# Next queries and negated maxima turned inside the running head; last gathers with fewer blankings

## What is computed

```
x = _layernorm(x + _L0_attn_ref(x, Wq, Wk, Wv, Wo))            # causal, 16 query heads on 4 key heads of 16, rope
x = _layernorm(x + _L0_xattn_ref(x, ctx, ctx, mask, ...))      # 16 heads over 64 context rows, causal
x = _layernorm(x + _L0_ffn_ref(x, ...))                        # 8 experts of 256-1024-256, top 2, and a shared one
x = _layernorm(x + _L1_attn_ref(x, time_mix_k, ...))           # K, V, R; S = scan(state * decay + K); (R * (S * first + K) * V) @ Wo
x = _layernorm(x + _L1_xattn_ref(x, ctx, ctx, mask, ...))      # one head of 256 over 64 context rows
x = _layernorm(x + _L1_ffn_ref(x, ...))                        # 16 experts of 256-128-256, top 4, and two shared ones
```

## Time and profile before

| | us |
|---|---|
| median of 3 runs | 1320.81 |
| lowest and highest | 1320.22, 1320.89 |
| the profiled execution | 1321.61 |
| its span, first to last instruction | 1319.4 |

### The profile page before, as it was taken

How to read it: one execution, slowest core, us unless ns; L and a number is a source line. 1 busy time by engine, 2 the same in 40 slices (tenths; PEclk the granted TensorE clock), 3 DMA queues, 4 the chain that set the end, 5 groups by cost and what they waited for, 6 DMA issues and landing times. The chain is left out here.

```text
span 1319.4 us, 23829 instructions
## 1 busy us (share of the span) xinstructions
PE 1157.6 (88%) x7558; PEld 836.2 (63%) x7558; DVE 697.9 (53%) x1882; ACT 586.9 (44%) x1071; POOL 474.6 (36%) x948
## 2 busy tenths in 40 slices
PE   7799898999978868999999999998789769999970
PEld 4344444444344435889999999987455556999940
DVE  4766666766255643422222323267677637554664
ACT  3277677777755634222333333231443122557710
POOL 7355332231432331013332323211342265716456
PEclk9599999999988988999999999999798759999995
DMA  9900200000000007301111111040800014867633
GB/s 347 351 1 13 86 0 1 0 0 1 1 0 1 1 1 303 150 25 34 40 37 37 37 37 39 27 136 1 274 1 1 12 69 131 259 194 240 205 118 102
DMA packets 68128, 109.32 MB, mean 83 GB/s; under 512 B 7345, under 2 KB 54962, under 8 KB 65202
## 3 DMA queue, kind: packets, MB, share of 16 engines
q1 hardware_dynamic: 58130, 80.96, 18.0%
q0 software_dynamic: 9888, 27.01, 6.4%
HBM read 65.61 MB, written 42.34 MB: 82 GB/s over the span
## 5 line engine op out<-in xcount | busy, mean ns | idle before, releaser
L1421 ACT ACTIVATE f_work<-f_bank,f_ub 128x128 f32<-128x128 f32 x312 | 89.0, 368 | 204.3 <-PE f_bank L1743 204.3
L496 ACT ACTIVATE att_PT<-att_ST 128x1024 f32<-128x1024 f32 (+1 forms) x192 | 148.1, 809 | 64.2 <-PE att_ST L634 32.7
L541 DVE CUSTOM_DVE_ANT_0 att_junk<-att_RB,att_causal_q 128x128 f32<-128x128 f32 (+3 forms) x256 | 120.7, 488 | 58.0 <-PE att_RB L616 49.0
L1743 PEld LDWEIGHTS f_bank<-f_work,f_xTf 128*128 128x128 f32 x1248 | 145.3, 192 | 3.9 <-DVE f_work L1543 2.0
L1743 PE MATMUL f_bank<-f_work,f_xTf 128*128 128x128 f32 x1248 | 145.8, 275 | 1.5 <-DVE f_work L1543 1.5
L1752 PE MATMUL f_bank<-wd_down,f_work 128*128 x624 | 141.1, 379 | 0.0
L616 PE MATMUL att_RB<-att_kT,att_qT 96*128 96x512 bf16 (+3 forms) x384 | 120.4, 351 | 22.0 <-DVE att_mx L541 6.6
L1752 PEld LDWEIGHTS f_bank<-wd_down,f_work 128*128 128x128 f32 x624 | 115.5, 190 | 14.1
L1372 POOL DMA_INDIRECT Yd<-f_work,f_inv x39 | 38.5, 987 | 196.3 <-DVE f_work L1562 196.3
L1552 DVE COPY f_xTf<-wu_up 128x1024 f32 x78 | 54.1, 695 | 102.6 <-PE f_bank L1743 94.9
L616 PEld LDWEIGHTS att_RB<-att_kT,att_qT 96*128 96x128 bf16 x384 | 34.0, 98 | 112.9 <-issue 41.2
(11 more groups left out here) (460 smaller groups left out, 2188.1 us busy)
## 6 DMA issues: line engine op xcount, KB each, us to landing
Xd<-g_zero SPq DMA_DIRECT2D x1, 12032.0 KB, 41.2
f_xin<-Xd SPq DMA_DIRECT2D x47, 256.0 KB
Yd<-f_yo SPq DMA_DIRECT2D x47, 256.0 KB, 2.6
wu_up<-up_w SPq DMA_DIRECT2D x9, 1024.0 KB, 9.3
wd_down<-down_w SPq DMA_DIRECT2D x9, 1024.0 KB, 18.4
w_all<-w SPq DMA_DIRECT2D x6, 768.0 KB, 10.6
wu_up<-Yd SPq DMA_DIRECT2D x16, 256.0 KB, 6.0
w_all<-w SPq DMA_DIRECT2D x1, 2304.0 KB, 17.2
```

What stands on the lines that cost most here:

```text
L496: act.activation(buf[:, :, 0:w], ST[:, 2 * (k % 2):2 * (k % 2) + 2, 0:w], ACT.Exp, scale=float(HD) ** -0.5).then_inc(exp_done, 1)
L541: dve.tensor_tensor_reduce(junk[:, k % RING, 0:w], RB[:, bank, 0:w], G.causal_q[:, 512 - w:512], 1.0, LOWEST, ALU.add, ALU.max, to).then_i ...
L1421: last = act.activation(hT[:, u % 2, m, :], bank[:, UB + m // 4, (m % 4) * P:(m % 4 + 1) * P], ACT.Gelu, bias=ub[:, ds(e, 1), m])
L1743: mm = pe.matmul(bank[:, UB + n, P * m:P * (m + 1)], staged_up[:, kk, at:at + P], xT[:, u % 2, kk, :], start=(kk == 0), stop=(kk == KD - 1))
```

## The change

In the prologue of the self-attention, `trQ` of the next head now stands behind the fourth `mx` of the running head, and `trm` of the head before behind its eighth. In the last head `trK` takes the place of `trQ`. At the end only `trQ` 0 and `trm` 3 are left. All `tr` steps but the first two go to two banks of their own, which are the first two of `ST`; the maxima keep the ring of three. PE waits for the two banks to be read before the iterations start, and once for the input tiles that ACT reads from there.

In the recurrent stage `ct` moves between the two halves of `r` of the last quarter, `lc` and `sx` 0 to 3 directly behind `r`. `spread_of` loses two of four operations where only `rstd` is used. In the other cases the negation comes first and is not waited for.

In the second half of the last gathers a blanking stays only behind every second gather of tiles 0 to 2, so 26 of 32 go. `spread(1)` moves from behind tile 0 to behind tile 2, and `norm(1)` on DVE from ahead of tile 1 to ahead of tile 3.

```
-    PROLOGUE += [("trQ", _r or -REP)] + [("mx", 12 * _r + k) for k in range(12)]
+    _head = [("mx", 12 * _r + k) for k in range(12)]
     if _r:
-        PROLOGUE.append(("trm", _r - 1))
-PROLOGUE += [("trK", 0), ("trm", REP - 1), ("trQ", 0)]
+        _head.insert(8, ("trm", _r - 1))
+    _head.insert(4, ("trQ", _r + 1) if _r + 1 < REP else ("trK", 0))
+    PROLOGUE += _head
+PROLOGUE += [("trQ", 0), ("trm", REP - 1)]
...
+class Prologue(Placed):
...
+            kind = "mx" if what == "mx" or n < 2 else "tr"
+            bank = turns[kind] % RING if kind == "mx" else RING + turns[kind] % SPARE
...
+                            pe.wait_ge(v_read, RINGP + NT - 2)
...
+            for n in range(RING, RING + SPARE):
+                pe.wait_ge(bank_free[n], PRO.count[n])
...
-    put(("r", 3, 1), ("ct", 0, 0))
-    put(("rs", 3, 1), ("lc", 0, 0), ("sx", 0, 3))
+    put(("r", 3, 0), ("ct", 0, 0))
+    put(("r", 3, 1), ("lc", 0, 0), ("sx", 0, 3))
...
-                ch.link(pool.tensor_tensor(rstd[n][p][:, j], rstd[n][p][:, j], half[:, j], ALU.pow))
-                ch.link(pool.tensor_tensor(shift[n][p][:, j], mv[n][p][:, j, 0], rstd[n][p][:, j], ALU.mult))
-                pool.tensor_scalar(shift[n][p][:, j], shift[n][p][:, j], -1.0, None, ALU.mult).then_inc(rstd_ready[n], 1)
+                if n == 1:
+                    pool.tensor_tensor(rstd[n][p][:, j], rstd[n][p][:, j], half[:, j], ALU.pow).then_inc(rstd_ready[n], 1)
+                else:
+                    ch.done(pool.tensor_scalar(shift[n][p][:, j], mv[n][p][:, j, 0], -1.0, None, ALU.mult))
+                    ch.link(pool.tensor_tensor(rstd[n][p][:, j], rstd[n][p][:, j], half[:, j], ALU.pow))
+                    pool.tensor_tensor(shift[n][p][:, j], shift[n][p][:, j], rstd[n][p][:, j], ALU.mult).then_inc(rstd_ready[n], 1)
...
-                        ch.pause(route.rest[:, 0:16])
-                    if n and s == 0:
+                        if n == 0 or (s < 3 and r % 2):
+                            ch.pause(route.rest[:, 0:16])
+                    if n and s == 2:
                         spread(1)
...
-                if s == 1:
+                if s == 3:
                     norm(1)
```

More of the change, by code:

```diff
@@ L172 @@
 PLAN = iteration_plan()
-PROLOGUE = [("trK", -1)]
+PROLOGUE = [("trK", -1), ("trQ", -REP)]
 for _r in range(REP):
-    PROLOGUE += [("trQ", _r or -REP)] + [("mx", 12 * _r + k) for k in range(12)]
+    _head = [("mx", 12 * _r + k) for k in range(12)]
     if _r:
-        PROLOGUE.append(("trm", _r - 1))
-PROLOGUE += [("trK", 0), ("trm", REP - 1), ("trQ", 0)]
+        _head.insert(8, ("trm", _r - 1))
+    _head.insert(4, ("trQ", _r + 1) if _r + 1 < REP else ("trK", 0))
+    PROLOGUE += _head
+PROLOGUE += [("trQ", 0), ("trm", REP - 1)]
 PLAN_6 = [x for x in PLAN if x not in (("trK", 0), ("trQ", 0))]
@@ L181 @@
 TRANSPOSES = ("trm", "trK", "trQ", "otr")
-RING = 3
+RING, SPARE = 3, 2
 class Placed:
@@ L219, in looped, with __init__ @@
     return placed
-PRO = Placed(PROLOGUE, [0] * RING)
-MID = Placed(PLAN, PRO.after())
+class Prologue(Placed):
+    def __init__(self, plan):
+        self.plan, self.base, self.at, self.count = plan, [0] * (RING + SPARE), [], [0] * (RING + SPARE)
+        turns = {"mx": 0, "tr": 0}
+        for n, (what, k) in enumerate(plan):
+            kind = "mx" if what == "mx" or n < 2 else "tr"
+            bank = turns[kind] % RING if kind == "mx" else RING + turns[kind] % SPARE
+            turns[kind] += 1
+            self.count[bank] += 1
+            self.at.append((bank, self.count[bank]))
+PRO = Prologue(PROLOGUE)
+MID = Placed(PLAN, PRO.after()[:RING])
 SIX = Placed(PLAN_6, MID.after(6))
@@ L228, in iteration @@
 def iteration(i):
-    return looped(PLAN, i, RING, TRANSPOSES + ("mx",), PRO.after())
+    return looped(PLAN, i, RING, TRANSPOSES + ("mx",), PRO.after()[:RING])
 def attention_stage(nc, a, G, y_sb, X):
@@ L274, in attention_stage @@
     rden = [sb(f"rden{p}", [P, 4, REP]) for p in range(2)]
-    RB = ps("RB", [P, RING, 512])
-    RBb = [RB[:, n, :].bitcast(BF16) for n in range(RING)]
-    ST = ps("ST", [P, 4, 512])
+    RB = ps("RB", [P, RING + 4, 512])
+    RBb = [RB[:, n, :].bitcast(BF16) for n in range(RING + SPARE)]
+    ST = RB[:, RING:RING + 4, :]
     OT = ps("OT", [P, 512])
@@ L282, in attention_stage @@
     v_ready, negm_ready = sem("v_ready"), sem("negm_ready")
-    bank_ready = [sem(f"bank_ready{n}") for n in range(RING)]
-    bank_free = [sem(f"bank_free{n}") for n in range(RING)]
+    bank_ready = [sem(f"bank_ready{n}") for n in range(RING + SPARE)]
+    bank_free = [sem(f"bank_free{n}") for n in range(RING + SPARE)]
     row_done = sem("row_done")
```

## The result

| | before | after |
|---|---|---|
| median, us | 1320.85 (4 runs, 1320.22 to 1322.16) | 1311.2 (4 runs: 1307.45, 1310.8, 1311.61, 1311.67) |
| the profiled execution, us | 1321.61 | 1311.67 |
| its span, us | 1319.4 | 1309.4 |
| PE busy, us | 1157.6 | 1154.0 |
| POOL busy, us | 474.6 | 466.9 |

A forecast was written before the change was run, and what follows sets the result against it. No single engine was taken as the bound, but chains across engines, with POOL late in the recurrent stage and last gathers. -0.5 - 7.6 + 0.5 - 4.9 = -12.5 us from 1320.8 gave 1308.3 us, range 1303.0 to 1312.5.

The forecast's parts named there:

- Prologue, -0.5: Self-attention prologue: three heads at 7.8 us give -1.2, the scores' start +0.3; half of the 0.9 us counted.
- The reason that I gave for the clock: Prologue: PE has 5.8 us of work in 7.8 us, still a gap in each head, so the clock stays 0.50.
- the rival of 1303.4: Prologue: denser PE work raises the clock, giving -5.4 instead of -0.5 us, total 1303.4 us; chance 0.12.
- Recurrent stage, -7.6: Recurrent stage: earlier places and shorter `spread_of` give -5.1 in the last quarter, -2.2 in earlier quarters, -0.3 at the end.
- my lower end of -5.5: Recurrent stage: gain of only 5.5 us if the granted clock is less kind in two or three windows.
- The earlier quarters: -2.2.: Recurrent stage, three earlier quarters: the second `x4` waits less for POOL, saving 0.73, 0.78 and 0.77 us.
- `lc` now starts when the scores have been taken off.: Recurrent stage, last quarter: `lc` starts near 1035.4 instead of 1039.17, so POOL's scatters end 3.8 us earlier.
- The two last `spread_of`: -0.3.: Recurrent stage, ahead of the final `x5`: each of the two last `spread_of` saves 0.15 us.
- Start of the last sublayer, +0.5: Between recurrent stage and last gathers: the low-clock stretch need not end earlier; an estimated +0.5 us.
- Last gathers, -4.9: Last gathers: `spread(1)` loses its 2.2 us wait, and 26 blankings fewer at 0.10 us each give -2.7 us.
- 1311.0: Last gathers: removing blankings gives nothing, as each gather waits for the one before; -2.2 there, total 1311.0 us; chance 0.13.
- 1346.6: Last gathers: gathers without blankings stall on each other, costing 35.6 us, total 1346.6 us; chance 0.03.

The follow-up runs named there:

- places alone: The kernel before with only the new places of `ct`, `lc` and `sx` in the recurrent stage; measured 0.9973 of before.
- `spread_of` alone: The kernel before with only the shorter `spread_of`; measured 0.9991 of before.
- filled: The changed kernel with products that nobody reads put into PE's waits of the recurrent stage; measured 0.9925 of before.
- `ct` moved: The changed kernel with `ct` ahead of both halves of `r` instead of between them; measured 0.9918 of before.
- prologue alone: The kernel before with only the change's reordering in the prologue of the self-attention; measured 1.000 of before.
- gathers alone: The kernel before with only the change's part on the last gathers; measured 0.9964 of before.
- recurrent alone: The kernel before with only the recurrent stage's part, the new order and the shorter `spread_of`; measured 0.9938 of before.
- after, again: The changed kernel, unaltered, run once more in the first group of follow-ups on another chip; measured 0.9904 of before.
- five banks: The changed kernel with the prologue's maxima on five banks instead of three; measured 0.9907 of before.
- after, third: The changed kernel, unaltered, run once more in the last group of follow-ups; measured 0.9906 of before, six runs from 1313.66 to 1322.01 us.
- five banks, no blanking: The changed kernel with five banks for the prologue's maxima and no blanking in the last 32 gathers; measured 0.9883 of before, median 1314.26 us.
- second look at before: Meant as the kernel before without 26 blankings, but it did not test that and served as a repeat of before; measured 0.9997.

## Why the prediction came out as it did

The recurrent stage over the profiles, in us. Steps: from POOL's first difference to the second `x4` of quarter 0; on to that of quarter 1; of quarter 2; to the first scatter; to the second `x4` of quarter 3; to the last `x5`. In brackets the us at half clock. The four runs that change or split the recurrent part are left out; their sums are 140.1 (47.9) with the places alone, 141.2 (55.9) with `spread_of` alone, 134.9 (42.8) filled and 139.4 (57.5) with `ct` moved.

| profile | to q0 | to q1 | to q2 | to scatter | to q3 | to x5 | sum |
|---|---|---|---|---|---|---|---|
| before | 28.38 | 26.59 (0) | 27.84 (6.8) | 29.08 (10.9) | 10.81 | 19.68 | 142.4 (50.2) |
| prologue alone | 28.26 | 26.62 (0) | 26.75 (3.4) | 30.61 (14.7) | 10.84 | 19.69 | 142.8 (50.6) |
| gathers alone | 28.82 | 26.61 (0) | 27.85 (6.8) | 29.03 (11.5) | 10.84 | 19.69 | 142.8 (50.7) |
| after | 27.83 | 25.89 (0.5) | 28.04 (9.8) | 27.70 (13.7) | 9.54 | 19.64 | 138.6 (56.7) |
| recurrent alone | 27.80 | 28.59 (6.8) | 26.90 (6.8) | 25.88 (10.2) | 9.54 | 19.64 | 138.4 (53.0) |
| after, again | 28.33 | 25.89 (0) | 25.45 (3.4) | 25.42 (7.1) | 10.45 | 19.60 | 135.1 (46.4) |
| five banks | 27.90 | 28.59 (6.8) | 26.90 (6.8) | 25.88 (10.2) | 9.54 | 19.64 | 138.5 (53.1) |
| after, third | 27.52 | 25.89 (0.5) | 28.05 (9.8) | 27.71 (13.7) | 9.57 | 19.64 | 138.4 (56.4) |
| five banks, no blanking | 27.91 | 25.88 (0.5) | 28.04 (9.8) | 27.71 (13.7) | 9.56 | 19.64 | 138.8 (56.8) |

- **Prologue, -0.5: right within what can be told, in part by luck.** The stalls are 0.43 and 0.85 us for two of 0.8, and the head takes 7.67 for 7.8: the three heads give -1.5 where -1.2 stood. The last `rowmax` to the first exponent takes 5.81 for 4.98 us, +0.8 where +0.3 stood. My chain to the end of ACT's copy was right (3.9 us), but PE starts the scores only 1.0 us behind it, at 66.29, and the row names no releaser. The two misses nearly cancel: -0.71 at the first exponent where -0.9 stood. That half of it would be left was not tested; the profiles differ by more. The reason that I gave for the clock was misread: PE had 6.9 us of work in a head of 8.54, not 5.8, and waited at most 1.2 us at a time. The 2.34 us are DVE's wait. After the change it is 6.7 in 7.67. The clock stayed at 0.50 even so, and the rival of 1303.4 did not come for this kernel. Its earlier release of the clock came with five banks, in both profiles. The Trainium skill ("TensorE: Matmul & The Clock Gate", Part 1) has the half clock as the default that sustained activity releases; these two profiles agree, since in the prologue only the ring was changed and PE became denser by it. But one of the profiles with three banks had 1.00 from 42.1 to 45.5 us with the prologue's instructions unchanged, so density is not all of it.
- **Recurrent stage, -7.6: mis-sized, as far as the profiles show.** The six profiles with it have a mean of 137.95 us, the four without it (those above and the second look at before) 142.59: -4.6 us, and -3.7 in the first pair. That is less than my lower end of -5.5. The ratios of its two halves add up to -4.8 us; only the ratio of the part alone, -8.2 with 2.8 either way, speaks for the full size. Three steps failed.
  - *"The earlier quarters: -2.2."* The lengths behave as forecast: quarter 1 takes 25.89 for 26.60 us, and at equal clock quarter 2 takes 26.90 for 27.84. (The second `x4` still waits 0.61 us for POOL, where I had named 0.2 as the sign; POOL itself waits 0.5 us for the moments of its second spread.) With 0.5 in quarter 0 these are the 2.2. But over quarters 1 and 2 together the six have a mean of 54.0 us and the four 54.2. Of 1.65 us won at equal clock the clock took back 1.5. The profile taken for the result had 56.7 us of the stage at 0.50, before 50.2. I had put that only into the bound, as two or three windows.
  - *"`lc` now starts when the scores have been taken off."* It starts when `ct` is there, 1.48 us later, as `ct` stands behind the first half of `r`. The run with `ct` moved shows it. With 1.0 and 0.7 us less at half clock the scatter came 2.9 and 3.2 us earlier, not 3.8.
  - *"The two last `spread_of`: -0.3."* The last step takes 19.64 for 19.68 us. Not seen.
  - Right: the shorter `spread_of` behind the scatters, 9.54 for 10.81 us, -1.3, in five of the six profiles.
- **Start of the last sublayer, +0.5**: 0.2 us in the first pair. The other chips cannot check it; on one of them the stretch differs by almost 4 us from kernel to kernel.
- **Last gathers, -4.9: right**, 43.13 for 48.02 us. The wait of `spread(1)`, 2.2 us, is gone, but the spread itself takes 1.9 us for 1.6, so 1.8 are left in its step from gather to gather (3.03 for 4.85). The other 3.1 come from the gathers without blankings. Most of those take 1.25 to 1.26 us from start to start, and 1.34 to 1.35 with a blanking; 26 times that difference is 2.3 to 2.6, where my sum has 2.7. Runs of twelve do not stall, so the rivals of 1311.0 and 1346.6 us fall. That the two shares separate is read from the rows; the run that should have split them did not.
- **Not in my sum**: 0.84 us at the start, which are chance and helped the forecast.

The terms give -0.71 - 3.7 + 0.2 - 4.9 - 0.84 = -9.95 us, the 10.0 of the spans. The forecast as a ratio is 0.9905. On two other chips the change gave 0.9904 and 0.9906, 12.8 and 12.5 us with about 3 either way, in the first comparison 0.9919; the three intervals overlap, and all hold the forecast. How much of the missing 2.9 us is the mis-sized term, and how much the draw of four runs, stays open. It also stays open why denser work in quarters 1 and 2 has more half clock, not less.

## What to carry to other kernels

In a stage where PE's granted clock changed to and fro, gains of 1.65 us on other engines left 0.2 on average here: look at several profiles of such a stage, with the us at each clock beside its length, before a term of 1 us is trusted. A ring of banks sets how long another job may stand between two of its users; two more banks were worth 5 us at the first exponent and 3.4 to 3.9 at the recurrent stage, where the reordering had given 0.7 at the first exponent. When a step is moved forward, ask what it will wait for in its new place, here 1.48 us for `ct`.

## What the runs showed of the hardware

The same instructions at the same stage took 135.1 to 138.8 us, with 46 to 57 us at half clock, and the patterns repeat to 0.01 us: three profiles show 28.04 and 27.70, two 28.59 and 26.90. That looks like a few discrete outcomes rather than noise. The Trainium skill ("TensorE: Matmul & The Clock Gate", Part 1) says that the activity monitor runs free of the kernel, so that one kernel can meet it at different points; the different patterns of one kernel, 138.6, 135.1 and 138.4 us for the stage, fit that, and the spread of its runs (1313.66 to 1322.01 us) may be its effect, though no run here fixed that point on purpose. That filling PE's waits raised the clock for the transposes and hardly moved the first gather was not expected either.
